# Scoring two head pairs at a time over four banks, projecting four pairs at a time, and a new order for the row

## Chip, cores and metric

The kernel runs on one core of one Trainium2 chip. The metric is the device time of one execution in microseconds (us). Engines are named as the profile names them: PE is TensorE, DVE VectorE, ACT ScalarE, POOL GpSimd, SP SyncE.

## The reference, cut to what matters

```python
x = L0_attn_x                                     # 16 rows (batches) of 256 tokens x 128
xn = _layernorm(x, axis=-1)
x = x + attention(xn) + experts(xn)
# attention: 16 heads of 8 channels
qkv = x @ Wqkv + bqkv
qf, kf = features(q), features(k)                 # normalised, times omega, clipped, exp: 64 features a head
ctx = einsum('bhtf,bhtfd->bhtd', q, cumsum(k v))  # causal linear attention
den = maximum(einsum(q, cumsum(k)), 1e-6)
out = (ctx / den) @ Wout + bout
# experts: 512 slots
logits = einsum('bsd,etd->bset', xn, se)
slots = softmax over tokens of logits, transposed, @ xn
processed = gelu(slots @ w1) @ w2
out = softmax over slots of logits @ processed
```

## The kernel before

One batch of 256 tokens is a *row* of the program; 16 rows are worked through, two of them before a hardware loop (`Fori`), twelve in it and two behind it (`run_rows`). Every engine has its instructions written out by hand in a function `row(b, first, nxt, nxt2)`; semaphores join them. `b` is the row, `bp` the one before, `b1` and `b2` the next two. Nothing reorders them: the order in which `row` is written is the order of each engine.

The causal attention is computed as scores: keys' features times queries' features, for eight *pairs* of heads a row (`scores(b, p)`, p from 0 to 7). One pair takes eight matmuls on a quarter of the array each (64 rows by 64 columns); head 0 of the pair goes to bank 0 of `p_s`, head 1 to bank 1. DVE takes bank 0 out with the causal mask (`evac_a`), ACT takes bank 1 out (`evac_b`), and POOL masks that one (`mask_b`). Then `context(b, a)` multiplies the scores with the values, on 128 by 32 tiles, into the last 128 columns of `p_s`; `ctx_copy`, `ctx_transposed`, `ctx_norm`, `attn_back`, `attn_copy`, `attention_out` and `add_attention` finish the attention.

`project(b, g)` makes the arguments of the features for two pairs, with fp16 operands on 64 by 128 tiles, into banks `p_f` and `p_g`; DVE clips them into `arg` (`clip`), ACT takes their exponential into `feat` (`feature_exp`), which has four places.

The expert part runs through four banks `x01` and `x23`: `logits_tokens`, `token_maxima`, `logits_turned`, `slot_maxima`, `shift`, `dispatch_exp`, `slot_sums`, `slots_norm`, `slots_transposed`, `slots_high` and `slots_low`, `hidden`, `gelu`, `processed`, `proc_copy`, `combine`, `add_experts`. They are full 128 by 128 matmuls, all but the bf16 ones of `shift` in fp32 or in an fp32 split in two. The layer norm and the qkv product of the next row use `x01` too.

In the row before the change one pair is scored at each of eight steps `s`, and a piece of the other work stands between one pair and the next:

```python
for s in range(8):
    ...
    scores(b, s)
    if s == 0:
        ... ctx_transposed(bp); qkv_product(b1)
    if s == 1:
        combine(bp); attn_back(bp)
```

Of the kernel before, what the change touches and what calls it, by code (L numbers as in the profile page):

```python
# [68 lines left out]
def step(b, k):  # L69

    i, u = b
    u += k
    return (i + u // 2, u % 2)

# [12 lines left out]
def build(nc, x, Wqkv, bqkv, Wout, bout, omega, nodes, weights, gamma_x, gamma_slot, slot_embeds,  # L87
          w1, w2, out):
    with ExitStack() as ctx:
# [81 lines left out]
        ffn_res = sb("ffn_res", [128, TILES, C])  # L171
# [112 lines left out]

        def load_omega(eng, a):
# [30 lines left out]
        def _(sp):  # L316
# [41 lines left out]
            load_x((0, 1), T)  # L358
            sp.wait_ge(om_zero, 1)
            load_omega(sp, 0)  # L360
            load_omega(sp, 1)
            spread(gs_bc, gamma_slot, C).then_inc(d_se, 16)
            sp.dma_start(se_rows[:, :, :], slot_embeds.rearrange("(c p) d -> p c d", p=128)).then_inc(d_se, 16)
# [9 lines left out]
            def row(b, first, nxt, nxt2):  # L373
                if nxt2:
                    load_x(step(b, 2), place(b, 2))
                if not first:
                    store(step(b, -1), place(b, -1))
                if nxt:
                    turn_stack(step(b, 1))

            run_rows(sp, row)
            store((B // 2 - 1, 1), (B - 1) * T)
# [7 lines left out]
        def _(pool):  # L390
# [63 lines left out]
            def row(b, first, nxt, nxt2):  # L454
                b1 = step(b, 1)
                for s in range(8):
                    if s == 2 and nxt:
                        squares(pool, b1)
                    if s == 4 and nxt:
                        qk_apply(pool, b1)  # L460
                    if s == 5 and nxt:
                        stack_low(pool, b1)
                    mask_b(b, s)
                    if s == 2 and nxt:
                        residual(b1)
                        place_v(b1)

            run_rows(pool, row)


        @block.scalar
        def _(act):
# [10 lines left out]
            def xt_high(b):  # L483
                after(act, tr_ok, count(b, 1, 1))
                nc.scalar.activation(xt_hi[:, b[1], :], x01[:, 0, 0:T], ACT.Copy).then_inc(xth_ok, 1)
# [17 lines left out]
            def evac_b(b, p):  # L503
                after(act, sb_ok, count(b, 8, p + 1))
                after(act, cx_ok, count(b, 4, p // 2 - 3))
                nc.scalar.activation(s_sb[:, p, 1, :], p_s[:, 1, 0:384], ACT.Copy).then_inc(eb_ok, 1)  # L506

            def ctx_copy(b, g):
                after(act, cx_ok, count(b, 4, 2 * g + 2))
                after(act, ct_ok, count(b, 1, 0))  # L510
                nc.scalar.activation(ctx_sb[:, g, :].rearrange("p (j t) -> p j t", j=TILES), p_s[:, :, 384:512],
# [24 lines left out]
            def proc_copy(b):  # L536
                after(act, pr_ok, count(b, 1, 1))
                nc.scalar.activation(proc[:, :, 0:C], x01[:, 1, :], ACT.Copy).then_inc(prs_ok, 1)  # L538
# [21 lines left out]
            qk_root(b0)  # L560

            stack_high(b0)
            nc.scalar.activation(stacked(2), parted(), ACT.Copy).then_inc(stcp_ok, 1)
# [5 lines left out]
            ln_root(b1)  # L569
# [3 lines left out]
            nc.scalar.activation(small[:, CT_, 8:12], small[:, CT_, 4:8], ACT.Exp, scale=-0.5).then_inc(se_a, 1)  # L573
            act.wait_ge(f_ok, 1)

            def row(b, first, nxt, nxt2):

                b1, b2, bp = step(b, 1), step(b, 2), step(b, -1)
                for s in range(8):
                    if s == 0:  # L580
                        if first:
                            feature_exp(b, 0)
                            act.wait_ge(se_t, 1)
                            nc.scalar.activation(se_hi[:, :], x23[:, 0, :], ACT.Copy).then_inc(se_h, 1)
                            feature_exp(b, 1)
                            xt_high(b1)
# [610 lines left out]
```

## Time and profile before

| | |
|---|---|
| median of 3 runs | 502.74 us (502.51 to 503.14) |
| time of the profiled execution | 502.99 us |
| span in its profile, first to last instruction | 501.0 us |
| PE busy | 466.5 us (93%) |
| DVE busy | 373.2 us (74%) |
| ACT busy | 312.8 us (62%) |
| POOL busy | 173.8 us (35%) |

The span is shorter than the time, since what lies around the first and the last instruction isn't in it. A PE busy time is modelled at its ends, so the start of a block of matmuls against the start of the next tells more than the sum.

### The profile page before, as it was taken

Reading aid. Unit: us, or ns where it says so; the run is one execution under the profiler, and the core shown is the slowest. Engines: PE = TensorE matmul, PEld = TensorE weight load, DVE = VectorE, ACT = ScalarE, POOL = GpSimd, SP = SyncE. Lnnn points to the kernel's source line nnn. Section 1 sums busy time; section 2 is a strip of 40 time slices with the busy share of each in tenths; the row PEclk is TensorE's granted clock in tenths of the full one; section 3 lists DMA queues with packets and bytes.
Section 4 is the critical chain, followed back from the end, with each engine's and each line's share of the span. In section 5 each row is a group of like instructions: output and inputs, shape, how many; then the busy total and the mean of one; then the engine's idle time right before and its main releaser. Section 6 shows DMA issues by size and latency. Waiting matters only on the chain.

```text
span 501.0 us, 15989 instructions
## 1 busy us (share of the span) xinstructions
PE 466.5 (93%) x5716; PEld 368.2 (73%) x5716; DVE 373.2 (74%) x985; ACT 312.8 (62%) x545; POOL 173.8 (35%) x277
## 2 busy tenths in 40 slices
PE   4559999999999999999999999999999999999996
PEld 2236777878777787877778787777778787777775
DVE  3887777787868778786877878787777878785651
ACT  3343848576574847667484766758485675758561
POOL 4324143341615334251523425161442426143210
PEclk9977999999999999999999999999999999999999
DMA  2500303040020202011020202002020200202000
GB/s 61 134 0 4 53 12 54 1 56 13 16 50 10 52 6 57 0 32 31 10 52 10 52 0 52 11 10 52 10 52 0 58 5 10 44 12 43 12 3 10
DMA packets 45779, 14.46 MB, mean 29 GB/s; under 512 B 35640, under 2 KB 45624, under 8 KB 45752
## 3 DMA queue, kind: packets, MB, share of 16 engines
q1 hardware_dynamic: 45176, 13.77, 13.9%
q8 instruction: 17, 0.28, 0.2%
q10 hardware_dynamic: 576, 0.33, 0.2%
q14 instruction: 10, 0.08, 0.1%
HBM read 3.61 MB, written 2.10 MB: 11 GB/s over the span
## 4 chain that ended last, share of the span: by engine, by line
PE 80%; DVE 9%; issue 5%; ACT 4%; DMA 1%; ACTq 0%; DVEq 0%
PE x L920 17%; PE p_s L958 14%; PE x L1074 13%; PE x L1085 6%; PE x L1047 6%; PE p_s L976 6%; PE p_f L945 4%; PE x L1019 4%; DVE log_sb L738 3%; ACT disp L521 3%; PE x L1030 3%; DVE arg L704 2%; PE x L999 2%; PE x L1055 2%; PE x L987 2%
## 5 line engine op out<-in xcount | busy, mean ns | idle before, releaser
L442 POOL TENSOR_TENSOR s_sb<-s_sb,causal 128x256 f32<-128x256 f32 x128 | 94.2, 736 | 281.9 <-ACT s_sb L506 281.9
L710 DVE TENSOR_TENSOR s_sb<-p_s,causal 128x384 f32<-128x384 f32 x128 | 71.2, 556 | 63.2 <-PE p_s L958 60.7
L958 PEld LDWEIGHTS p_s<-feat 64*64 64x64 f32 x2048 | 78.6, 134 | 35.9 <-issue 29.1
L958 PE MATMUL p_s<-feat 64*64 64x256 f32 (+3 forms) x2048 | 100.8, 313 | 1.1 <-DVE s_sb L710 1.1
L506 ACT ACTIVATE s_sb<-p_s 128x384 f32<-128x384 f32 x128 | 62.5, 488 | 50.8 <-PE p_s L958 50.2
L501 ACT ACTIVATE feat<-arg,f_bias 128x512 f32<-128x512 f32 x128 | 88.2, 713 | 4.3 <-DVE arg L704 4.3
L1074 PE MATMUL x<-w_sb,hid_t 128*128 128x128 f32 x512 | 65.7, 281 | 0.0
L704 DVE TENSOR_SCALAR arg<-p_f,f_low,f_high 128x512 f32<-128x512 f32 x64 | 51.6, 806 | 18.1 <-PE p_f L945 18.0
L1074 PEld LDWEIGHTS x<-w_sb,hid_t 128*128 128x128 f32 x512 | 59.6, 191 | 7.1 <-issue 7.0
L704 DVE TENSOR_SCALAR arg<-p_g,f_low,f_high 128x512 f32<-128x512 f32 x64 | 51.4, 803 | 0.0
L976 PE MATMUL p_s<-s_sb,vw 128*32 128x128 f32 x1536 | 48.6, 274 | 0.2
L976 PEld LDWEIGHTS p_s<-s_sb,vw 128*32 128x32 f32 x1536 | 40.3, 110 | 7.1 <-DVE s_sb L710 3.6
L475 ACT ACTIVATE small<-small 128x4 f32<-128x4 f32 (+1 forms) x32 | 7.4, 231 | 46.2 <-DVE small L691 39.8
L1047 PE MATMUL x<-xg,disp 128*128 128x129 f32 x256 | 32.8, 281 | 3.0 <-ACT disp L521 3.0
L1047 PEld LDWEIGHTS x<-xg,disp 128*128 128x128 f32 x256 | 29.8, 191 | 5.4 <-ACT disp L521 5.4
L1085 PE MATMUL x<-proc,comb_t 128*128 128x129 f32 x256 | 32.9, 281 | 0.2 <-ACT proc L538 0.2
L533 ACT ACTIVATE hid_t<-x 128x1024 f32<-128x1024 f32 x32 | 32.6, 1020 | 0.0
L1085 PEld LDWEIGHTS x<-proc,comb_t 128*128 128x128 f32 x256 | 29.8, 191 | 1.7 <-ACT proc L538 0.5
L945 PE MATMUL p_f<-stack_t,omega_st 64*128 64x512 f16 x64 | 24.5, 383 | 6.9 <-DVE arg L704 3.8
L920 PE MATMUL x<-slot_hi,w_hi 128*128 128x512 f32 x64 | 28.6, 447 | 0.0
L738 DVE TENSOR_SCALAR_CACHE_REDUCE log_sb<-x 128x512 f32<-128x512 f32 x32 | 21.4, 690 | 5.4 <-PE x L920 5.4
L920 PE MATMUL x<-slot_hi,w_lo 128*128 128x512 f32 x64 | 25.4, 397 | 0.0
(135 smaller groups left out, 798.4 us busy)
## 6 DMA issues: line engine op xcount, KB each, us to landing
out_dram<-out_sb SPq DMA_DIRECT2D x32, 64.0 KB, 2.1
xin<-in_L_attn_x_dram SPq DMA_DIRECT2D x31, 64.0 KB, 2.4
omega_f<-in_L_attn_omega_dram SPq DMA_DIRECT2D x16, 4.0 KB
se_rows<-n_L_ffn_slot_embeds_dram SPq DMA_DIRECT2D x1, 256.0 KB, 4.1
w_f<-in_L_ffn_w_dram SPq DMA_DIRECT2D x1, 256.0 KB, 4.3
w_sb<-in_L_ffn_w_dram SPq DMA_DIRECT2D x1, 256.0 KB, 4.7
stack_t<-stack SPq DMA_TRANSPOSE x16, 4.4
wqkv_f<-in_L_attn_Wqkv_dram SPq DMA_DIRECT2D x1, 192.0 KB, 3.9
```

Source lines behind the costliest of these rows:

```text
L442: pool.tensor_tensor(v, v, m, ALU.mult).then_inc(mb_ok, 1)
L501: nc.scalar.activation(feat[:, p % 4, :], arg[:, p % 4, :], ACT.Exp, bias=f_bias[:, 0:1]).then_inc(fe_ok, 1)
L506: nc.scalar.activation(s_sb[:, p, 1, :], p_s[:, 1, 0:384], ACT.Copy).then_inc(eb_ok, 1)
L704: nc.vector.tensor_scalar(arg[:, p % 4, :], bank[:, :], f_low[:, 0:1], f_high[:, 0:1], ALU.max, ALU.min).then_inc(cl_ok, 1)
L710: nc.vector.tensor_tensor(s_sb[:, p, 0, :], p_s[:, 0, 0:384], causal[:, :], ALU.mult).then_inc(ea_ok, 1)
L920: mm = nc.tensor.matmul(dst, a, w, start=start and i == 0, stop=stop and i == 2, skip_group_check=True)
L945: nc.tensor.matmul(bank[:, :], omega_st[rows, g, :], stack_t[rows, b[1], :, :, g, :].rearrange("p j k t -> p k j t"), start=True, stop=Tru ...
L958: mm = nc.tensor.matmul(p_s[rows:rows + 64, u, o:o + hi - lo], f[:, T + keys:T + keys + 64], f[:, lo:hi], start=True, stop=True, skip_grou ...
L976: mm = nc.tensor.matmul(p_s[32 * q:32 * q + 32, j, 384:512], vw[:, b[1], kt, QUADS * a + q, :], s_sb[:, p, q % 2, o:o + 128], start=(kt == ...
L1047: mm = nc.tensor.matmul(x01[:, half, 129 * (c % 2):129 * (c % 2) + 129], disp[:, j, 128 * c:128 * c + 128], xg[:, b[1], j, :], start=(j == ...
L1074: mm = nc.tensor.matmul(x01[:, 1, 128 * c:128 * c + 128], hid_t[:, m, 128 * c:128 * c + 128], w2_sb[:, m, :], start=(m == 0 and c == 0), s ...
L1085: mm = nc.tensor.matmul(x23[:, 0, 129 * j:129 * j + 129], comb_t[:, c, 128 * j:128 * j + 128], proc[:, c, :], start=(c == 0), stop=(c == N ...
```

## The change

Banks `p_f` and `p_g` go; in their place stands a second pair of score banks, `p_t`. Even pairs are scored into `p_s`, odd ones into `p_t`, two pairs one behind the other. Two projections also stand one behind the other, into the same four banks. Contexts go to `p_s`, `x23` or `x01` (`home`). The row now begins with the logits, the last two pairs of a row are scored in the next row, its contexts also; the experts of a row are finished in the row itself. `dispatch_exp` and `proc_copy` are cut in two halves, the qkv product goes to `x23`, results wait in a doubled `ffn_res`, and stores go out a row later. The start has its loads and steps in another order, and the layer norm of row 0 no longer stands behind the wait for the bias rows (`d_rows`).

```diff
-        p_f = pb("p_f", [128, 512])
-        p_g = pb("p_g", [128, 512])
         p_s = pb("p_s", [128, 2, 512])
+        p_t = pb("p_t", [128, 2, 512])
...
+        def home(b, g):
+
+            if g == 1:
+                return x23
+            return x01 if is_row(b, B - 1) else p_s
...
             def dispatch_exp(b):
-                after(act, shd_ok, count(b, 1, 1))
-                nc.scalar.activation(disp[:, :, :], x01[:, :, :], ACT.Exp).then_inc(ed_ok, 1)
+                for j in range(TILES):
+                    after(act, shd_ok, count(b, 2, j + 1))
+                    nc.scalar.activation(disp[:, j, :], x01[:, j, :], ACT.Exp).then_inc(ed_ok, 1)
...
             ln_stats(b0)
-            dve.wait_ge(d_rows, 32)
             ln_apply(b0)
...
             def project(b, g):
                 after(pe, d_st, count(b, 16, 16))
-                hold(pe, cl_ok, count(b, 8, 2 * g))
-                for u, (bank, done) in enumerate(((p_f, ft_ok), (p_g, fg_ok))):
+                if g == 0:
+                    hold(pe, ea_ok, count(b, 8, -1))
+                    hold(pe, eb_ok, count(b, 8, -1))
+                    hold(pe, cs_ok, count(b, 2, -1))
...
+                else:
+                    hold(pe, ea_ok, count(b, 8, g + 1))
+                    hold(pe, eb_ok, count(b, 8, g + 1))
...
             def scores(b, p):
                 after(pe, fe_ok, count(b, 8, p + 1))
-                after(pe, ea_ok, count(b, 8, p))
-                hold(pe, eb_ok, count(b, 8, p))
-                if p in (0, 6):
-                    hold(pe, cs_ok, count(b, 2, p // 6))
+                if p in (0, 1, 4, 5):
+                    hold(pe, cl_ok, count(b, 8, (2, 4, 0, 0, 6, 8)[p]))
+                else:
+                    hold(pe, ea_ok, count(b, 8, p - 1))
+                    hold(pe, eb_ok, count(b, 8, p - 1))
+                dst = (p_s, p_t)[p % 2]
...
-                for s in range(8):
...
+                logits_tokens(b, nxt)
+                if first:
+                    transposes(b1)
+                else:
+                    scores(bp, 6)
+                    scores(bp, 7)
+                logits_turned(b)
+                if not first:
+                    lump_low(bp, False)
+                shift(b)
+                if first:
+                    pe.wait_ge(om_s, 3)
+                project(b, 0)
+                project(b, 1)
+                slot_sums(b, 0)
+                slot_sums(b, 1)
+                if nxt:
+                    qkv_product(b1)
+                slots_transposed(b)
+                scores(b, 0)
+                scores(b, 1)
+                if not first:
+                    lump_high(bp, nxt, False)
+                if first:
+                    pe.wait_ge(w1_split, 2)
+                    pe.wait_ge(d_late, 16 * LATE)
+                hidden(b, first, 0)
+                hidden(b, first, 1)
+                scores(b, 2)
+                scores(b, 3)
+                processed_low(b)
+                if not first:
+                    ctx_transposed(bp)
+                project(b, 2)
+                project(b, 3)
+                processed_high(b)
+                if not first:
+                    attn_back(bp)
+                combine(b)
+                if not first:
+                    attention_out(bp)
+                if nxt2:
+                    transposes(b2)
+                scores(b, 4)
+                scores(b, 5)
```

`lump_low` is `context(b, 0)` and `context(b, 1)` with their waits, `lump_high` is `context(b, 2)` and `context(b, 3)`. `processed_low` and `processed_high` are the two halves of `processed`.

Two places show what moves. On PE before, inside a row of the loop, the second half of `processed` (L1074) stands ahead of pair 0 (the four rows of L958), and behind it the context transposes of the previous row (L987).

```order
L1074 MATMUL x01<-w2_sb,hid_t 128x128 x8
L53 REGISTER_ALU
L958 MATMUL p_s<-feat 64x256 x2
L958 MATMUL p_s<-feat 64x192 x2
L958 MATMUL p_s<-feat 64x64 x2
L958 MATMUL p_s<-feat 64x128 x2
L987 MATMUL x23<-ident,ctx_sb 128x128 x4
```

On PE of the change, from the end of pair 2 on: L989 are the matmuls of a pair (pair 3 goes to `p_t`), L1136 the first half of `processed`, L1043 the context transposes, L974 the projections.

```order
L989 MATMUL p_s<-feat 64x128 x2
L989 MATMUL p_t<-feat 64x256 x2
L989 MATMUL p_t<-feat 64x192 x2
L989 MATMUL p_t<-feat 64x64 x2
L989 MATMUL p_t<-feat 64x128 x2
L53 REGISTER_ALU
L1136 MATMUL x01<-w2_sb,hid_t 128x128 x8
L53 ISA
L53 REGISTER_ALU
L1043 MATMUL x23<-ident,ctx_sb 128x128 x4
L974 MATMUL p_s<-stack_t,omega_st 128x512 x2
L974 MATMUL p_t<-stack_t,omega_st 128x512 x2
```

Two pairs of heads now have nothing between them, and the projections stand two and two.

On DVE before, in the loop, the context normalisation of the previous row (L717 to L729) stands between two evacuations (L710), and the clips (L704) are spread over the row.

```order
L710 TENSOR_TENSOR s_sb<-p_s,causal 128x384
L53 ISA
L717 TENSOR_SCALAR den<-x 128x2x4x2 x2
L722 RECIPROCAL rden<-den 128x32
L53 REGISTER_ALU
L729 TENSOR_TENSOR attn<-x,rden 128x2x32 x4
L710 TENSOR_TENSOR s_sb<-p_s,causal 128x384
```

On DVE of the change the same normalisation (L744 to L756) stands ahead of four clips in a row (L730), the experts' sum (L796, L800), the low half of the transposed tokens (L698), the final addition (L808) and the evacuations of pairs 4 and 5 (L736).

```order
L756 TENSOR_TENSOR attn<-x,rden 128x2x32 x4
L53 REGISTER_ALU
L730 TENSOR_SCALAR arg<-p_s,f_low,f_high 128x512 x2
L53 REGISTER_ALU
L730 TENSOR_SCALAR arg<-p_t,f_low,f_high 128x512 x2
L796 RECIPROCAL comb_rs<-x 128x2
L800 SCALAR_TENSOR_TENSOR ffn_res<-x,comb_rs,xres 128x128 x2
L53 ISA
L698 TENSOR_TENSOR xt_lo<-x,xt_hi 128x256
L53 REGISTER_ALU
L808 TENSOR_TENSOR out_sb<-x,ffn_res 128x256
```

What was spread over the eight steps of a row now stands in one run of DVE, behind the normalisation.

## Rows read from the trace of the kernel before

**Rows 1.** The page, busy times by engine, and the chain by engine.

```profile
PE 466.5 (93%) x5716; PEld 368.2 (73%) x5716; DVE 373.2 (74%) x985; ACT 312.8 (62%) x545; POOL 173.8 (35%) x277
...
PE 80%; DVE 9%; issue 5%; ACT 4%; DMA 1%; ACTq 0%; DVEq 0%
```

**Rows 2.** Windows: length; PE, PEld, DVE, ACT, POOL busy; granted clock; DMA.

```profile
32.50:42.80 10.30, 8.05 (x61) 6.22 (x61) 6.55 (x14) 2.98 (x7) 4.41 (x8) 0.50 0.01 2
...
231.55:260.36 28.81, 28.21 (x357) 22.49 (x358) 22.66 (x60) 19.21 (x34) 10.51 (x16) 1.00 0.13 27
```

**Rows 3.** Timeline of PE, in one row of the loop: start, length, instructions.

```profile
241.20 0.77 PE L958 MATMUL p_s<-feat 64*64 64x256 f32 x16
241.90 0.71 PE L999 MATMUL x<-wout_sb,attn_t 128*128 128x128 f32 x4
...
243.60 0.40 PE L920 MATMUL x<-se_hi,xt_lo 128*128 128x512 f32 x1
243.93 0.77 PE L958 MATMUL p_s<-feat 64*64 64x256 f32 x16
244.80 1.09 PE L1019 MATMUL x<-ident,log_sb 128*128 128x128 f32 x8
245.82 0.39 PE L945 MATMUL p_f<-stack_t,omega_st 64*128 64x512 f16 x1
...
246.24 0.40 PE L1030 MATMUL x<-neg_ident,maxima 128*128 128x128 bf16 x4
...
247.38 0.77 PE L958 MATMUL p_s<-feat 64*64 64x256 f32 x16
...
251.79 1.52 PE L976 MATMUL p_s<-s_sb,vw 128*32 128x128 f32 x48
253.24 0.50 PE L920 MATMUL x<-slot_hi,w_hi 128*128 128x512 f32 x1
253.57 0.39 PE L920 MATMUL x<-slot_lo,w_hi 128*128 128x512 f32 x1
253.80 0.40 PE L920 MATMUL x<-slot_hi,w_lo 128*128 128x512 f32 x1
...
258.16 2.05 PE L1074 MATMUL x<-w_sb,hid_t 128*128 128x128 f32 x16
260.05 0.38 PE L928 MATMUL x<-ident,xg 128*128 128x128 f32 x2
260.36 0.39 PE L945 MATMUL p_f<-stack_t,omega_st 64*128 64x512 f16 x1
...
260.68 1.52 PE L976 MATMUL p_s<-s_sb,vw 128*32 128x128 f32 x48
```

**Rows 4.** Timeline of DVE, in the same row of the loop.

```profile
257.96 0.56 DVE L710 TENSOR_TENSOR s_sb<-p_s,causal 128x384 f32<-128x384 f32 x1
258.43 0.80 DVE L704 TENSOR_SCALAR arg<-p_f,f_low,f_high 128x512 f32<-128x512 f32 x1
259.15 0.80 DVE L704 TENSOR_SCALAR arg<-p_g,f_low,f_high 128x512 f32<-128x512 f32 x1
```

**Rows 5.** Timeline of ACT: the load of the other activation table.

```profile
259.43 1.28 ACT L622 ACT_TABLE_LOAD   x1
```

**Rows 6.** Waits of PE from 60 to 460 us: total, times, longest.

```profile
PE p_f L945 <- DVE arg L704: 3.8, 12, 0.4
```

**Rows 7.** Timeline of DVE at the start.

```profile
8.18 0.16 DVE L636 SCALAR_TENSOR_TENSOR small<-small 128x4 f32<-128x4 f32 x1 [3.50 <-DMA bqkv_bc<-in_L_attn_bqkv_dram]
```

**Rows 8.** Timeline of SP at the start: the omega loads.

```profile
8.59 5.64 SPq L292 DMA_DIRECT2D omega_f<-in_L_attn_omega_dram  x16
```

**Rows 9.** The line of the slot transposes: durations, first and last start.

```profile
L1055 PE MATMUL x<-ident,slot_v x64: 272/273/330, 49.2 to 481.3; 128*128 128x128 f32 x64
```

**Rows 10.** Timeline of PE in the last row: slot transposes and context transposes.

```profile
480.90 0.66 PE L1055 MATMUL x<-ident,slot_v 128*128 128x128 f32 x4
...
492.94 0.60 PE L987 MATMUL x<-ident,ctx_sb 128*128 128x128 f32 x4
```

More of the change, by code:

```diff
@@ L376, in row @@
                 if not first:
-                    store(step(b, -1), place(b, -1))
-                if nxt:
-                    turn_stack(step(b, 1))
+                    turn_stack(b)
+                if not first and not is_row(b, 1):
+                    store(step(b, -2), place(b, -2))
             run_rows(sp, row)
-            store((B // 2 - 1, 1), (B - 1) * T)
+            for u in range(2):
+                store((B // 2 - 1, u), (B - 2 + u) * T)
             for u in range(2):
@@ L681, in qkv_bias @@
                     after(dve, qkv_ok, count(b, 2, j + 1))
-                    last = nc.vector.scalar_tensor_tensor(qkv[:, j, :], x01[:, j, 0:384], small[:, SG, j:j + 1],
+                    last = nc.vector.scalar_tensor_tensor(qkv[:, j, :], x23[:, j, 0:384], small[:, SG, j:j + 1],
                                                           bqkv_bc[:, :], ALU.mult, ALU.add)
@@ L840, in _ @@
             last.then_inc(se_ok, 1)
-            clip(b0, 0)
-            clip(b0, 1)
+            ln_stats(b1)
+            dve.wait_ge(om_s, 2)
+            for u in range(2):
+                o = 64 * u
+                last = nc.vector.tensor_tensor(omega_st[o + 32:o + 48, :, :], omega_f[o:o + 16, :, :],
+                                               omega_st[o:o + 16, :, :], ALU.subtract)
+            last.then_inc(om_s, 1)
+            dve.wait_ge(f_ln, 1)
+            nc.vector.tensor_tensor(f_bias[:, :], coef_ln[:, :], node_c[:, :], ALU.subtract).then_inc(f_ok, 1)
@@ new lines, in row @@
+                evac_a(b, 1)
+                if nxt:
+                    qk_norms(b1)
+                    qk_newton(b1)
+                if nxt2:
+                    ln_apply(b2)
+                if nxt:
+                    stack_again(b1)
+                evac_a(b, 2)
+                evac_a(b, 3)
+                if not first:
+                    ctx_norm(bp)
+                clip(b, 4)
+                clip(b, 5)
+                clip(b, 6)
+                clip(b, 7)
+                add_experts(b)
@@ L1023, in logits_turned, with shift @@
                         mm.then_inc(lt_ok, 1)
-            def shift(b, h):
-                after(pe, mx_ok, count(b, 2, h + 1))
-                for c in (2 * h, 2 * h + 1):
-                    for j in range(TILES):
+            def shift(b):
+                after(pe, mx_ok, count(b, 2, 2))
+                for j in range(TILES):
+                    for c in range(NCH):
                         mm = nc.tensor.matmul(x01[:, j, 128 * c:128 * c + 128],
@@ L1056, in slots_transposed, with hidden @@
                 mm.then_inc(slt_ok, 1)
-            def hidden(b, nxt, half):
+            def hidden(b, first, half):
                 if half == 0:
@@ L1061, in hidden @@
                     after(pe, slh_ok, count(b, 1, 1))
+                elif not first:
+                    after(pe, cs_ok, count(b, 2, 0))
                 else:
-                    after(pe, ec_ok, count(b, 1, 1))
+                    pe.wait_ge(qkvs_ok, 2)
                 for m in (2 * half, 2 * half + 1):
@@ L1097, in _ @@
             qkv_product(b0)
-            pe.wait_ge(sthi_ok, 1)
-            for u in (0, 1, 0, 1, 0, 1):
-                nc.tensor.matmul(p_s[:, u, 0:384], ident[:, :], s_sb[:, 0, 0, :], start=True, stop=True)
-            pe.wait_ge(om_s, 3)
-            project(b0, 0)
             pe.wait_ge(se_ok, 1)
             for c in range(NCH):
-                mm = nc.tensor.transpose(x23[:, 0, 128 * c:128 * c + 128], se_n[:, c, :], ident[:, :])
+                mm = nc.tensor.transpose(x01[:, 1, 128 * c:128 * c + 128], se_n[:, c, :], ident[:, :])
```

477 lines of the change are left out of this document (230 added, 247 removed).

## The prediction

> **What bounds the kernel now.** I read the page first: PE is busy for 93% of the span and is 80% of the chain that ended last [rows 1]. The windows show one row of the loop, 28.81 us long: PE is busy 28.21 us of it at the full clock, DVE 22.66, ACT 19.21, POOL 10.51 [rows 2]. PE's waits are small: for the clips 3.8 us in all between 60 and 460 us [rows 6]. So the kernel is PE's list of blocks, 16 times over, and only what shortens that list or empties it can move the time. From the slot transposes of the first row (49.2, [rows 9]) to those of the last (480.9, [rows 10]) are 15 periods of 28.78 us.
>
> The timeline of PE tells what a block costs beside its columns [rows 3]. A run of 128 by 128 matmuls goes at a steady step: 16 instructions from 258.16 to 260.05, 1.89 us for 8 matmuls of 128 columns, 1.84 ns a column with the start. But each time the kind of tile changes there is a loss. The first split matmul behind a context takes 0.33 us (253.24 to 253.57), the next 0.23: entering costs 0.10. The last one ahead of a pair takes 0.33 too (243.60 to 243.93): leaving costs 0.10 (rounded down to 0.09 in the sums). A row of before has 25 such changes of kind, since eight pairs, four projections and two contexts all stand apart in the full-width work; a row of the change has 15.
>
> **The sum for a row.** The same matmuls run, so I lay their measured pieces end to end in the new order. Pieces that have a row [rows 3]: turned logits 1.02 (244.80 to 245.82), shift 1.14 (246.24 to 247.38), a context of two groups 1.45 (251.79 to 253.24), a lone pair of heads 0.70 (241.20 to 241.90), a lone projection 0.32 (260.36 to 260.68). The others follow from 0.235 for a 512-column split instruction, three quarters of it for a 384-column one, 0.11 for half a fp32 matmul of 128 columns, and 0.10 each for entering and leaving.
> - logits 1.60; turned 1.02; context 1.45; shift 1.14
> - slot sums, qkv product, slot transposes in one run: 1.78 + 1.04 + 0.44 + 0.19 = 3.45
> - context 1.45; both hidden halves in one run, 12 x 0.235 + 0.19 = 3.02
> - first half of processed with context transposes, 1.78 + 0.44 + 0.19 = 2.42 (rounded up)
> - second half, attention back, combine, attention out, transposes: 1.78 + 0.22 + 1.78 + 0.45 + 0.22 + 0.19 = 4.64
>
> Together 20.19 us. To it come four double pairs and two double projections. The trace never shows two blocks of one kind with a wait between them, so the second block's price is bounded. For a pair: below, the lone block without its two ends, 0.70 - 0.19 = 0.51; above, everything paid again, 0.70 + 0.19 = 0.89. Each quarter of the array streams 320 columns in a pair (256 + 64, 192 + 128), at 1.84 ns 0.59 us; I take 0.60. For a projection: below 0.13, above 0.51; 512 columns in one pass are the 0.23 of a split instruction, which I take. So 4 x (0.70 + 0.60) + 2 x (0.32 + 0.23) = 6.30, and the row is 26.5 us.
>
> The Trainium skill (TensorEngine Tiling (Array Packing), Key Properties) says that a change of tiling mode drains TensorE and that going to another tile of one mode does not. The 0.10 on either side agree with it; by it the second block of a pair pays nothing, which is the 0.60, while with both switches paid again the sum would be 502 (worked out below).
>
> **Who is late next.** I walked the other engines through this row from its logits (0), with DVE steps of 0.47 for an evacuation and 0.72 for a clip [rows 4], 1.28 for each of the two table loads [rows 5], and what the same line took before for the rest. One place makes PE wait. The slot sums need both halves of the dispatch exponential, done at 7.0, and run to 8.95; DVE, with three clips ahead (to 9.1) and then both normalisations (to 10.3), frees the slot transposes only at 10.4, when the qkv product, which covers 1.0 of it, has ended at 10.0. That is 0.4 us a row. Elsewhere the cover holds, thinly: fourth clip 11.0 for pair 1 at 11.6; qkv bias 12.1 for the context at 12.25, where the array goes into `x23`; evacuation of pair 3 at 19.7 for the projection at 20.5, behind a table load and both GELUs on ACT; proc halves 22.5 and 23.7 for the combine at 23.2 and 24.0; all four later clips 24.8 for pair 5 at 26.3; pair 5 out of its bank 1.2 us into the next row, for pair 7 at 2.2. POOL and SP are not near: the stack of a row goes out at 19.2 of the row before and has some 14 us until its projections. Splitting the dispatch exponential and the proc copy costs ACT one more small start each, within its idle time of 9.6 us (28.81 - 19.21, [rows 2]). So the row is 26.93 us, and 15 periods are 404.0 against 431.7. Three joints with 0.1 to 0.3 us in hand will slip at times; for these I add 0.2 a row, 3 us in all.
>
> **The two ends.** Start: the norm of row 0 no longer waits for the bias rows, 3.5 us of DVE idle [rows 7]. The logits no longer stand behind the first projections and their transposing DMA, but behind the normalised slots. The sixteen omega loads took 5.64 us to issue [rows 8]; they now start some 3.5 us earlier, ahead of the load of the second row, so the slot rows are asked for at about 11 and land at about 15. Behind that stand on ACT their squares and both roots, on DVE the query and key norms, the stack and the normalised slots, at 21.7 by their lengths; then the transposes and the warm-up matmuls, so the logits start at about 26 and the slot transposes at 35.4, one row's chain later, with waits; I say 37, since part of it may run at half clock, as 32.5 to 42.8 us does now [rows 2]. Before it was 49.2 [rows 9]. Tail: before, 20.1 us from the last slot transposes to 501.0 [rows 10]. Now almost all of the attention lies behind them: 1.30 + 1.45 + 3.02 + 1.30 + 2.42 + 0.55 + 4.4 + 1.30 for the rest of the row, 1.45 and 1.30 for the first contexts and pairs 6 and 7, 0.55 for the slot transposes, 1.5 for the last evacuation and mask, 1.45 for the last context, 0.6 for its copy, and 7.4 from the context transposes on (8.06 from 492.94 to 501.0, less 0.7 since the combine isn't between): 30.1.
>
> **Sum:** 37.0 + 404.0 + 3.0 + 30.1 = 474.1 us of span. The profiled execution lasted 502.99 us with a span of 501.0, so 2.0 us lie around it: 476 us. Its time is 0.25 above the median of 502.74, which I leave out.
>
> **Rivals.**
> - *The evacuations bind* (0.20). DVE must put 22.66 us into 26.9, and what was spread over eight steps stands in one run: context normalisation, four clips, experts' sum, low half, addition, evacuations. If DVE keeps the scattered idle of before, 28.81 - 22.66 = 6.15, nothing is won; if half of what should go (1.9 us) stays, the row is 27.9 and the time 491. For it: 0.1 to 0.5 us in hand at several joints. Against: each wait here is for work that is one block old. The Trainium skill (TensorEngine Tiling (Array Packing), PSUM Bottleneck) warns that with a tiled array the copies out of PSUM may become the limit, and asks for both engines on it, as both kernels have; it would give this case.
> - *The change doesn't save its switches* (0.07). If the wait ahead of the second block lets the array run empty, each second pair costs 0.89 and each projection 0.51: 15 x (4 x 0.29 + 2 x 0.28) = 26 us, time 502, no change; half of it gives 489. Against: the conditions are usually met before the wait is reached.
> - *The clock falls* (0.06), the slower side. In 32.5 to 42.8 us PE was busy 8.05 of 10.3 us and granted 0.50 of its clock [rows 2]. If the wait ahead of the slot transposes brought that on, a microsecond there would do half the work. The 27 us forecast are eaten by about 54 us at half clock, 3.6 a row; one stretch of 5 us a row would give 476 + 15 x 2.5 = 514. Against: in the loop the full clock is granted [rows 2], and the new wait is 0.4 us.
>
> **How the numbers follow.** The forecast case has 0.67 and spans 468 (second pair at 0.51, no slips: 4 x 0.09 x 15 + 3 = 8 less) to 484 (second pair 0.7 and another slip of 0.1 a row). The range takes in most of the evacuation case: 468 to 492. About 0.2% tells from no change. Faster is the forecast case, the evacuation case and most of the second rival: 0.91; same 0.03; slower 0.06.
>
> **What would show it.** In the profile after: slot transposes 26.9 to 27.2 apart; the second pair starts 0.70 behind the first and the next kind 0.60 behind that; PE's waits led by the slot transposes for `slot_v`, some 6 us; first slot transposes near 37. Wrong, if PE's waits for `s_sb`, `arg` or `feat` exceed 10 us, if the clock shows 0.5 inside the loop, or if the second pair takes 0.8 or more.

## The result

| | before | the change |
|---|---|---|
| median | 502.84 us (502.51 to 503.14, 4 runs) | 474.38 us (474.12 to 476.84, 4 runs) |
| profiled execution: time, span | 502.99, 501.0 us | 476.84, 475.1 us |

The ratio is 0.9445 [0.9418, 0.9472]: 28.5 us less. The forecast was 476 us, in a range of 468 to 492. The profiled execution of the change is the slowest of its four, 2.5 us above their median, and everything read from the profile below is from that one.

### The profile page after: what moved, and what is told of

Read it like the earlier page. It is cut to its first block, busy times and chain, and to the rows that moved or that the text cites. A ratio compares the mean times of both kernels' runs of the same rounds, so it can differ in the third digit from the quotient of the medians.

```text
span 475.1 us, 16056 instructions
## 1 busy us (share of the span) xinstructions
PE 438.9 (92%) x5712; PEld 361.6 (76%) x5712; DVE 388.5 (82%) x985; ACT 307.0 (65%) x578; POOL 171.1 (36%) x277
## 4 chain that ended last, share of the span: by engine, by line
PE 80%; DVE 12%; issue 4%; SPq 2%; DMA 1%; ACT 1%; DVEq 0%
PE x L936 16%; PE p_s L989 9%; PE p_t L989 7%; PE x L1136 7%; PE x L1145 7%; PE x L1157 6%; DVE arg L730 6%; PE x L1001 5%; PE p_s L1001 5%; PE x L1079 3%; DVE slot_v L785 3%; PE p_s L974 2%; PE x L1114 2%; PE x L1090 2%; PE x L1055 2%
## 5 line engine op out<-in xcount | busy, mean ns | idle before, releaser
L730 DVE TENSOR_SCALAR arg<-p_s,f_low,f_high 128x512 f32<-128x512 f32 x64 | 48.8, 803 | 18.0 <-PE p_s L974 18.0
L989 PEld LDWEIGHTS p_s<-feat 64*64 64x64 f32 x1024 | 38.6, 132 | 18.2 <-issue 16.6
L730 DVE TENSOR_SCALAR arg<-p_t,f_low,f_high 128x512 f32<-128x512 f32 x64 | 50.0, 801 | 0.0
L989 PE MATMUL p_s<-feat 64*64 64x256 f32 (+3 forms) x1024 | 49.5, 309 | 0.0
L989 PE MATMUL p_t<-feat 64*64 64x256 f32 (+3 forms) x1024 | 46.1, 296 | 0.0
L527 ACT ACTIVATE s_sb<-p_s 128x384 f32<-128x384 f32 x64 | 31.0, 484 | 21.2 <-PE p_s L989 21.2
L989 PEld LDWEIGHTS p_t<-feat 64*64 64x64 f32 x1024 | 41.5, 133 | 1.5
L736 DVE TENSOR_TENSOR s_sb<-p_s,causal 128x384 f32<-128x384 f32 x64 | 35.2, 550 | 6.6 <-PE p_s L989 5.8
L736 DVE TENSOR_TENSOR s_sb<-p_t,causal 128x384 f32<-128x384 f32 x64 | 35.1, 548 | 0.0
L1136 PE MATMUL x<-w_sb,hid_t 128*128 128x128 f32 x256 | 32.8, 281 | 0.0
L527 ACT ACTIVATE s_sb<-p_t 128x384 f32<-128x384 f32 x64 | 31.5, 493 | 0.7
L1136 PEld LDWEIGHTS x<-w_sb,hid_t 128*128 128x128 f32 x256 | 29.8, 191 | 1.2
```

Of the source, the lines that this page charges most:

```text
L527: nc.scalar.activation(s_sb[:, p, 1, :], (p_s, p_t)[p % 2][:, 1, 0:384], ACT.Copy).then_inc(eb_ok, 1)
L730: nc.vector.tensor_scalar(arg[:, p % 4, :], bank, f_low[:, 0:1], f_high[:, 0:1], ALU.max, ALU.min).then_inc(cl_ok, 1)
L736: nc.vector.tensor_tensor(s_sb[:, p, 0, :], (p_s, p_t)[p % 2][:, 0, 0:384], causal[:, :], ALU.mult).then_inc(ea_ok, 1)
L989: mm = nc.tensor.matmul(dst[rows:rows + 64, u, o:o + hi - lo], f[:, T + keys:T + keys + 64], f[:, lo:hi], start=True, stop=True, skip_grou ...
L1136: nc.tensor.matmul(x01[:, c // 2, o:o + 128], hid_t[:, m, 128 * c:128 * c + 128], w2_sb[:, m, :], start=(m == 0 and c % 2 == 0), stop=Fals ...
```

## The profile after

The page: busy times by engine, to be held against [rows 1].

```profile
PE 438.9 (92%) x5712; PEld 361.6 (76%) x5712; DVE 388.5 (82%) x985; ACT 307.0 (65%) x578; POOL 171.1 (36%) x277
```

PE has the same matmuls, less four instructions of warm-up at the start (which write nothing that is read), and is busy 27.6 us less. Nearly all of that is in the loop: 28.21 us busy in a row of before [rows 2], 26.39 in the row below. The columns are the same, so what went lies between the blocks of matmuls, where the profile counts it as busy. DVE has the same 985 instructions and is busy 15.3 us more. That is the line of this page to stop at: equal work that takes longer calls for a reason.

The line of the slot transposes (against [rows 9]; its last start is that of the row's last matmul), and then windows: most of one loop row, the stretch at half clock in the first row, and everything from the last row's slot transposes on.

```profile
L1114 PE MATMUL x<-ident,slot_v x64: 272/273/331, 39.0 to 444.9; 128*128 128x128 f32 x64
```

```profile
43.50:46.90 3.40, 3.40 (x9) 2.62 (x10) 2.62 (x9) 1.79 (x3) 0.73 (x2) 0.50 0.00 0
231.04:257.84 26.80, 26.39 (x356) 21.92 (x348) 23.52 (x61) 18.44 (x36) 10.14 (x16) 1.00 0.14 29
444.56:475.10 30.54, 22.76 (x360) 19.11 (x360) 12.49 (x33) 14.95 (x26) 5.66 (x8) 0.92 0.04 10
```

The first transposes start at 38.98 and the last row's at 444.56: 15 periods of 27.04 us, where before had 28.78. So the span is 38.98 + 405.58 + 30.54 = 475.1, and 1.7 us lie around it. The start is 10.2 us shorter than before and the tail 10.4 us longer, so by the profiles the whole gain of the span, 26 us, is in the rows.

PE's timeline in one row of the loop (start, length, instruction, in brackets the idle time before it), to be held against [rows 3].

```profile
235.24 0.77 PE L989 MATMUL p_s<-feat 64*64 64x256 f32 x16
235.84 0.72 PE L989 MATMUL p_t<-feat 64*64 64x256 f32 x16
236.49 2.05 PE L1136 MATMUL x<-w_sb,hid_t 128*128 128x128 f32 x16
238.38 0.60 PE L1043 MATMUL x<-ident,ctx_sb 128*128 128x128 f32 x4
239.13 0.39 PE L974 MATMUL p_s<-stack_t,omega_st 64*128 64x512 f16 x2 [0.16 <-issue]
239.59 0.39 PE L974 MATMUL p_t<-stack_t,omega_st 64*128 64x512 f16 x2
239.92 2.05 PE L1145 MATMUL x<-w_sb,hid_t 128*128 128x128 f32 x16
...
252.11 0.39 PE L974 MATMUL p_s<-stack_t,omega_st 64*128 64x512 f16 x2
252.33 0.38 PE L974 MATMUL p_t<-stack_t,omega_st 64*128 64x512 f16 x2
...
255.52 0.34 PE L936 MATMUL x<-wqkv_hi,xt_lo 128*128 128x384 f32 x1
256.01 0.66 PE L1114 MATMUL x<-ident,slot_v 128*128 128x128 f32 x4
256.59 0.77 PE L989 MATMUL p_s<-feat 64*64 64x256 f32 x16
```

Read the starts. Two pairs take 0.60 (235.24 to 235.84) + 0.65 (to 236.49) = 1.25 us. The slot transposes start 0.49 behind the last matmul of the qkv product, which steps at 0.18: a wait of 0.31. And projection 3 starts 0.46 behind projection 2 (239.13 to 239.59), where projection 1 starts 0.22 behind projection 0 (252.11 to 252.33). Projection 2 is late too. From the context transposes to the second half of `processed` it is 1.54 us here (238.38 to 239.92), and 1.07 in the kernel with the copy moved, below (260.42 to 261.49). That is a loss of 0.47 us in this row and 0.54 in the next, which the prediction does not have. The idle time in the brackets, 0.16, is less than the wait of projection 2, since PE's ends are modelled.

What makes these projections late? Projection 2 goes into `p_s` and waits for the evacuation of pair 2, projection 3 into `p_t` and waits for that of pair 3. Here is DVE at the same place of the next row, then ACT's evacuation of pair 3, and the two projections.

```profile
262.09 1.02 DVE L660 SCALAR_TENSOR_TENSOR small<-small 128x4 f32<-128x4 f32 x1 [0.22 <-DVE small L664]
...
264.51 1.06 DVE L777 COPY stack<-stack 128x512 f16<-128x512 f16 x1
265.50 0.55 DVE L736 TENSOR_TENSOR s_sb<-p_s,causal 128x384 f32<-128x384 f32 x1
265.97 0.54 DVE L736 TENSOR_TENSOR s_sb<-p_t,causal 128x384 f32<-128x384 f32 x1
...
265.12 0.51 ACT L527 ACTIVATE s_sb<-p_t 128x384 f32<-128x384 f32 x1
...
266.25 0.39 PE L974 MATMUL p_s<-stack_t,omega_st 64*128 64x512 f16 x2 [0.23 <-issue]
266.71 0.39 PE L974 MATMUL p_t<-stack_t,omega_st 64*128 64x512 f16 x2
```

Each projection starts 0.20 us behind the end of its evacuation on DVE (266.05 and 266.51). ACT's of pair 3 has ended at 265.63, 0.88 us earlier than DVE's. So it is DVE that holds them, and on DVE the copy of the stack (L777) stands right ahead.

POOL in that row:

```profile
262.01 1.08 POOL L313 TENSOR_TENSOR qk_n<-qkv,small 128x512 f32<-128x512 f32 x1 [1.55 <-DVE small L664]
264.27 1.16 POOL L321 TENSOR_TENSOR stack<-qk_n,stack 128x512 f16<-128x512 f32 x1 [1.18 <-ACT stack L516]
```

An operation on four elements a partition takes 1.02 us and ends when POOL's does (263.11 and 263.09). The fp16 copy takes 1.06 us, and ends 0.14 behind POOL's `stack_low`, which is running when it starts. It is so in 12 of the 15 copies (1.06 to 1.10 us; the first two and the last take 0.28 to 0.30) and in 12 of the 16 small operations. The twelve rows with a long copy have projections 2 and 3 at 0.46 to 0.49 us apart. The three with a short copy, and the last row, which has none, have them 0.22 to 0.23 apart. The groups by line, after:

```profile
L777 DVE COPY stack<-stack 128x512 f16<-128x512 f16 x15 | 13.9, 924 | 2.2 <-ACT stack L516 2.2
L660 DVE SCALAR_TENSOR_TENSOR small<-small 128x4 f32<-128x4 f32 x16 | 12.9, 809 | 3.2 <-DVE small L664 2.6 <-ACT small L497 0.5
```

And before, the same two operations:

```profile
L750 DVE COPY stack<-stack 128x512 f16<-128x512 f16 x15 | 5.2, 348 | 0.0
L636 DVE SCALAR_TENSOR_TENSOR small<-small 128x4 f32<-128x4 f32 x16 | 2.5, 154 | 3.7 <-DMA bqkv_bc<-in_L_attn_bqkv_dram 3.5 <-ACT small L477 0.2
```

8.7 and 10.4 us more: together more than all of DVE's growth, 15.3. The Trainium skill ("SBUF — State Buffer", Who interferes with whom) says that GpSimd and some operations of VectorE share an access to SBUF that one of them holds for its whole instruction. The trace agrees, with 1.02 us for an operation of 0.15 to 0.16, which starts 0.08 behind POOL's and ends with it.

The two operations also overlapped before, without a price for DVE. Here are the copy and POOL's `stack_low` in the row of [rows 3]:

```profile
250.09 0.28 DVE L750 COPY stack<-stack 128x512 f16<-128x512 f16 x1
...
250.23 1.16 POOL L310 TENSOR_TENSOR stack<-qk_n,stack 128x512 f16<-128x512 f32 x1 [0.32 <-ACT stack L495]
```

In 14 of 15 rows of before the copy starts 0.05 to 0.20 us ahead of POOL's and takes 0.28; in the one where POOL is ahead, by 0.05, it takes 1.25. In the twelve long rows of the change POOL is ahead by 0.21 to 0.25. So it is not the overlap that counts but which of the two starts first: against POOL's start the copy comes 0.3 to 0.45 us later in the change than before. (In two rows of the change POOL's start is recorded 0.02 ahead and the copy is still short.)

## The experiments

Each time is a median with its range; the ratio is to the kernel before, run beside it. "Row" is the period of the slot transposes.

### The pairs apart again

The change, with three of the four pairings undone; pairs 0 and 1 stay together.

```diff
                     scores(bp, 6)
-                    scores(bp, 7)
                 logits_turned(b)
                 if not first:
+                    scores(bp, 7)
                     lump_low(bp, False)
...
                 hidden(b, first, 0)
-                hidden(b, first, 1)
                 scores(b, 2)
+                hidden(b, first, 1)
                 scores(b, 3)
...
                 combine(b)
+                scores(b, 4)
                 if not first:
                     attention_out(bp)
...
-                scores(b, 4)
                 scores(b, 5)
```

> The change with three of the four double pairs taken apart: turned logits between pairs 6 and 7, the first hidden half... the second hidden half between pairs 2 and 3 (pair 2 stands between the two hidden halves), attention out and transposes between pairs 4 and 5. Banks, waits and matmuls are the same. Theory (the gain is the changes of tile kind saved): each adds one lone block, 0.19 us of entering and leaving and 0.65 to 0.70 in place of 0.60 behind the first, so 0.24 to 0.29 us each, three a row, 16 rows: 11.5 to 14 us slower than the change, 486 to 488 us. Rival (the gain came from waits that the new order hides, not from the tile kinds): within 2 us of the change.

Measured: 499.99 us (498.43 to 501.46), ratio 0.9945 [0.9922, 0.9968], row 28.53. That is 25.6 us against the change, twice what the theory had, and the rival doesn't have it either. PE's waits of this kernel between 60 and 440 us (total, times, longest) show why.

```profile
PE x L1090 <- DVE maxima L772: 5.8, 14, 0.4
PE x L936 <- DVE xt_lo L698: 2.5, 6, 0.4
PE x L936 <- issue: 1.9, 7, 0.3
```

The edit opened two waits: the shift for the maxima, 0.4 us a row, and the logits for `xt_lo`, 0.3 to 0.4 a row, since less PE work now stands ahead of both. So this run can't price a pairing. It was split in two further down.

### The copy behind the evacuations; the normalisations ahead of the clip; both

Three kernels, each the change with one or both of two moves on DVE. The copy of the stack is let past the two evacuations that projections 2 and 3 wait for:

```diff
-                if nxt:
-                    stack_again(b1)
                 evac_a(b, 2)
                 evac_a(b, 3)
+                if nxt:
+                    stack_again(b1)
```

> The change with the second copy of the stack on DVE (1.06 us here, 0.28 before) moved behind the evacuations of pairs 2 and 3. Theory: projections 2 and 3 wait about 0.4 us a row for DVE's evacuations of pairs 2 and 3, which stand behind that copy while POOL works; moving it frees them: 15 x 0.4 = 6 us faster than the change, about 468.5. Rival: ACT's evacuations of the same pairs, behind both GELUs, come as late, so at most 1.5 us faster. Second rival: what starts earlier stalls at the next joint, no change.

Measured: 468.90 us (468.75 to 470.28), ratio 0.9349 [0.9319, 0.9379], row 26.56, 5.5 us less than the change, as the theory had it (its row is 0.48 shorter, of which 0.07 is the half clock in the first row of the change, which this kernel did not have). PE's timeline at the projections:

```profile
260.95 0.39 PE L974 MATMUL p_s<-stack_t,omega_st 64*128 64x512 f16 x2
261.18 0.38 PE L974 MATMUL p_t<-stack_t,omega_st 64*128 64x512 f16 x2
261.49 2.05 PE L1145 MATMUL x<-w_sb,hid_t 128*128 128x128 f32 x16
```

They are 0.23 apart, and the next kind starts 0.31 behind: 0.54 for both. The copy itself fell too, since in most rows POOL's `stack_low` has ended when it comes, or ends within 0.03 us.

```profile
L777 DVE COPY stack<-stack 128x512 f16<-128x512 f16 x15 | 4.6, 307 | 0.0
```

The second move goes for the wait that the prediction did have:

```diff
                 clip(b, 1)
-                clip(b, 2)
                 slots_norm(b, 0)
                 slots_norm(b, 1)
+                clip(b, 2)
                 clip(b, 3)
```

> The change with both slot normalisations on DVE ahead of the third clip. Theory: the slot transposes no longer wait (0.32 us a row in the loop), the fourth clip comes 0.1 us later and pair 1 waits at most 0.15: 0.2 to 0.3 a row, 3 to 4.5 us faster, 470 to 471.5. Rival: pair 1 or the context behind it takes the whole wait over, since the fourth clip and the qkv bias are late next: no change within 1 us.

Measured: 476.76 us (475.78 to 478.58), ratio 0.9508 [0.9471, 0.9545], row 27.08: nothing won. The row is 0.04 longer, and the 2.4 us that the median is above the change's are no clear loss, since the ranges and the intervals of the two overlap. PE's timeline:

```profile
254.35 0.34 PE L936 MATMUL x<-wqkv_hi,xt_lo 128*128 128x384 f32 x1
254.53 0.60 PE L1114 MATMUL x<-ident,slot_v 128*128 128x128 f32 x4
255.05 0.78 PE L989 MATMUL p_s<-feat 64*64 64x256 f32 x16
255.88 0.78 PE L989 MATMUL p_t<-feat 64*64 64x256 f32 x16
256.84 1.52 PE L1001 MATMUL x<-s_sb,vw 128*32 128x128 f32 x48 [0.18 <-DVE qkv L707]
```

The transposes start at once (0.18), but pair 1 starts 0.83 behind pair 0 instead of 0.60, behind the clips, and the context waits for the qkv bias. DVE's work between the slot sums and that context is one sum; its order only chooses who stands at the end of it.

> Both of the DVE moves in one kernel. Theory: they stand at different joints and add up: 9 to 10.5 us faster than the change, 464 to 465.5. Rival: PE's list is at its floor of 26.5 us a row, so the sum of both can be no more than 15 x 0.55 = 8 us, 466.

Measured: 473.24 us (472.06 to 474.14), ratio 0.9418 [0.9387, 0.9449]. The steady row is 26.77, against 26.56 with the copy's move alone, so the second move costs 0.2 a row once the first is made; its first row also lasted 29.36 us, with 42.2 to 49.1 us at half clock, against 26.97. The gains don't add.

### The start, on the kernel with the copy moved

The warm-up matmuls left out (they write nothing that is read):

```diff
-            for u in (0, 1, 0, 1):
-                nc.tensor.matmul(p_s[:, u, 0:384], ident[:, :], s_sb[:, 0, 0, :], start=True, stop=True)
```

> The kernel with the stack copy moved (468.9 us), without the four warm-up matmuls ahead of row 0's logits. Theory (they only keep the array busy and are in the way): the low halves of the slots are done at 26.8 us and the logits start at 28.7 to 29.2, so 1.9 to 2.4 us faster, 466.7. Rival: the array is then granted half its clock in the first row, where a 512-column instruction steps 0.43 in place of 0.23 us, and the first row is longer by more than that: same or up to 5 us slower.

Measured: 469.73 us (467.76 to 470.09), ratio 0.932 [0.9279, 0.9362]. No difference from the kernel with them that these ranges can tell. PE's timeline without:

```profile
27.57 0.77 PE L936 MATMUL x<-se_hi,xt_hi 128*128 128x512 f32 x1 [2.29 <-issue]
28.14 0.63 PE L936 MATMUL x<-se_lo,xt_hi 128*128 128x512 f32 x1
28.56 0.63 PE L936 MATMUL x<-se_hi,xt_lo 128*128 128x512 f32 x1
```

And with them:

```profile
28.67 0.69 PE L936 MATMUL x<-se_hi,xt_hi 128*128 128x512 f32 x1
29.20 0.40 PE L936 MATMUL x<-se_lo,xt_hi 128*128 128x512 f32 x1
29.43 0.40 PE L936 MATMUL x<-se_hi,xt_lo 128*128 128x512 f32 x1
```

Without them the logits start 1.1 us earlier and step at 0.43, with them later and at 0.23. Either way the slot transposes come at about 38: at 38.6 without, at 38.1 with, and at 37.4 to 39.0 over all the kernels here that have the warm-ups. In this profile the first row without them also lasted 27.83 us, with half clock from 42.5 to 46.0, against 26.97; the change itself, with the warm-ups, had such a stretch too, so it can't be put down to them.

The wait for the bias rows put back where it was before the change:

```diff
             ln_stats(b0)
+            dve.wait_ge(d_rows, 32)
             ln_apply(b0)
```

> The kernel with the stack copy moved, with the wait for the bias rows put back ahead of the layer norm of row 0. Theory: the start now hangs on the slot rows, for which ACT waits until 16.7 us, and what is moved by 1.2 to 2.9 us at the start ends well before: no change, within 1 us of 468.9. Rival (the removed wait is part of the gain): 1.2 to 2.9 us slower.

Measured: 469.91 us (467.62 to 470.74), ratio 0.9339 [0.9303, 0.9376]. No difference, although the same wait was DVE's longest at the start before [rows 7].

### More work on DVE

One more clip a row (0.72 us, to a place that nobody reads) ahead of the eighth clip, on the kernel with the copy moved. It tests whether DVE's sum of work is near to binding.

```diff
+                if p == 7:
+                    nc.vector.tensor_scalar(junk[:, :, :].rearrange("p a c -> p (a c)"), bank, f_low[:, 0:1],
+                                            f_high[:, 0:1], ALU.max, ALU.min)
```

> The kernel with the stack copy moved, with one clip more a row on DVE (0.72 us, its result goes nowhere), ahead of the eighth. Theory (DVE has 1.0 to 1.4 us in hand at the end of a row): 0 to 0.2 a row, at most 3 us slower, 472. Rival (the evacuations bind): 16 x 0.72 = 11.5 us slower, 480.

Measured: 468.57 us (467.79 to 470.73), ratio 0.9321 [0.928, 0.9362], row 26.56. It costs nothing at that place. The stretch ahead of the slot transposes, where DVE is what PE waits for, isn't tested by it.

### Prices of single pairings, on the kernel with the copy moved

Half of `processed_high` (`processed_high(b, h)` does chunks 2h and 2h + 1) between the second two projections:

```diff
                 project(b, 2)
+                processed_high(b, 0)
                 project(b, 3)
-                processed_high(b)
+                processed_high(b, 1)
```

> The kernel with the stack copy moved, with the first half of the second half of processed between projections 2 and 3. Theory (a change of tile kind costs what it did for the pairs): a lone projection costs 0.32 in place of 0.22 and 0.19 for entering and leaving, 0.29 a row, 4.6 us slower, 473.5. Rival (the later projection makes clips, features and pair 5 late): 10 us or more slower, with waits of PE at pair 5 or at the next row's logits.

Measured: 473.45 us (472.3 to 474.97), ratio 0.9413 [0.937, 0.9457], row 26.85: 0.29 a row.

The second half of `hidden` between pairs 2 and 3:

```diff
-                hidden(b, first, 1)
                 scores(b, 2)
+                hidden(b, first, 1)
                 scores(b, 3)
```

> The kernel with the stack copy moved (468.9 us, row 26.55), with only pairs 2 and 3 taken apart by the second hidden half. Theory (of the 1.5 us a row that taking three pairs apart cost, 0.35 each is tile kinds: two lone pairs 1.41 with 0.19 more of entering and leaving, against 1.25 for a double one; the rest is waits at other joints): row 26.9, 5 us slower, 474. Rival (each separation costs a third of the 1.5): row 27.05, 7.5 us slower, 476.5.

Measured: 474.44 us (473.24 to 476.06), ratio 0.9447 [0.9406, 0.9488], row 26.89: 0.33 a row, with no other wait of note.

Pair 4 ahead of `attention_out` and the transposes:

```diff
+                scores(b, 4)
                 if not first:
                     attention_out(bp)
                 if nxt2:
                     transposes(b2)
-                scores(b, 4)
                 scores(b, 5)
```

> The same with only pairs 4 and 5 taken apart, attention out and the transposes of row b+2 between them. Theory: 0.35 of tile kinds, and the transposes now stand 0.7 us later, so xt_high and xt_low are late for the next row's logits: 0.35 + 0.4 a row, row 27.3, 11 us slower, 480, with PE waiting for xt_low. Rival (no such wait when only this one is apart): 5 us slower, 474.

Measured: 480.35 us (479.11 to 480.71), ratio 0.9556 [0.9524, 0.9589], row 27.26: 0.70 a row. The logits now wait for `xt_lo`, by PE's timeline:

```profile
246.71 0.49 PE L936 MATMUL x<-se_hi,xt_hi 128*128 128x512 f32 x1 [0.42 <-DVE xt_lo L698]
```

So 0.70 is a pairing of 0.3 and a wait of 0.4. With this and the run before it the first experiment is explained: three pairings at 0.34, 0.4 for the maxima and 0.4 for `xt_lo` make 1.8; of the projections' wait, by starts 0.47 and 0.54 in turn, 0.10 and 0.18 to 0.19 are left, so about 0.3 a row goes off, which leaves 1.5 against the 1.49 measured.

### Where the copy's price comes from

Moving the copy on DVE changed two things, its place and its neighbour on POOL. Two kernels keep DVE's list of the change and reorder POOL's alone. In the first the copy of v goes ahead:

```diff
-                    stack_low(pool, b1)
                     place_v(b1)
+                    stack_low(pool, b1)
```

> The change itself, DVE as it was, with POOL's placing of the values ahead of its low half of the stack, so that a copy and no two-input operation runs on POOL when DVE comes to the second stack copy. Theory (DVE's copy takes 0.92 us on average since it has to let POOL's two-input operation end): the copy takes about 0.3 us again, projections 2 and 3 no longer wait, about 5 us faster than the change, 469 to 470. Rival (it is its place in DVE's order, or the wait for ACT's stack, that costs): the copy still ends after 0.9 us or the projections still wait, within 1 us of 474.4.

Measured: 475.74 us (474.76 to 476.85), ratio 0.9477 [0.9431, 0.9522], row 27.03. POOL in this kernel:

```profile
262.58 0.77 POOL L446 COPY vw<-qkv 128x64 f32<-128x64 f32 x4
263.83 1.16 POOL L321 TENSOR_TENSOR stack<-qk_n,stack 128x512 f16<-128x512 f32 x1 [0.47 <-ACT stack L516]
```

and DVE:

```profile
264.06 1.07 DVE L777 COPY stack<-stack 128x512 f16<-128x512 f16 x1
```

The copy of v fell into time in which POOL had idled for ACT, so `stack_low` still starts just ahead of DVE's copy. The collision was not removed, and the run decides nothing. In the second, `stack_low` goes behind two masks that can only run once ACT's evacuations are there:

```diff
-                    stack_low(pool, b1)
                     place_v(b1)
                 mask_b(b, 2)
                 mask_b(b, 3)
+                if nxt:
+                    stack_low(pool, b1)
```

> This is the change as made, with GpSimd's list alone in another order: the copy of v, then the masks of pairs 2 and 3, and only behind them the low half of the query and key stack. VectorE's list stays as in the change, with its repeat of the stack's first half ahead of the evacuations of pairs 2 and 3. Nothing is then left for GpSimd to run at the moment when that copy comes. Theory (the copy is slow because it shares an access to SBUF with an operation of GpSimd): the copy falls from 924 ns to about 0.3 us, projections 2 and 3 start 0.22 apart without a wait, the row is about 26.65 and the time about 469 to 470 us. Rival (the copy's place in VectorE's own list, or its wait for ScalarE's half of the stack, is what costs): copy and time stay, 0.92 us and 474.4 us.

Measured: 470.75 us (468.02 to 471.27), ratio 0.9383 [0.9333, 0.9433], row 26.56. DVE's group of the copy, at its old place in DVE's list (one line further down in this file):

```profile
L778 DVE COPY stack<-stack 128x512 f16<-128x512 f16 x15 | 4.2, 283 | 2.2 <-ACT stack L517 2.2
```

POOL's timeline around the copy, which ran at 259.26:

```profile
257.78 0.77 POOL L446 COPY vw<-qkv 128x64 f32<-128x64 f32 x4
260.13 1.41 POOL L454 TENSOR_TENSOR s_sb<-s_sb,causal 128x256 f32<-128x256 f32 x2 [1.58 <-ACT s_sb L528]
261.50 1.17 POOL L321 TENSOR_TENSOR stack<-qk_n,stack 128x512 f16<-128x512 f32 x1
```

The copy takes 283 ns at the same place and with the same wait for ACT, because POOL runs nothing then; the projections are 0.23 apart (260.68 and 260.91) and the row is that of the kernel with the copy moved. The theory is right: the price of the copy was POOL's operation, not its place on DVE.

## Why the prediction was right, and where it was off

**What bounds the kernel** was right: PE's list of blocks. The row's own terms add up to 26.89 where the prediction writes 26.93, and the tail's to 30.0 where it writes 30.1; neither matters to the time. With the copy moved, PE is busy for 26.42 of a 26.60 us stretch of the loop.

**The second pair** was given 0.60 and the next kind 0.10 less than a lone pair. The second starts 0.60 behind the first, so the first doesn't pay the 0.10 that a lone pair pays on leaving, and the next kind starts 0.65 behind the second: 1.25 instead of 1.30 for both, 0.2 us a row. "The second pair starts 0.70 behind the first" was thus wrong by 0.10. A pairing saves 0.33 a row by the one run that undid one without opening a wait, a pairing of projections 0.29.

**The stall at the slot transposes** was given as 0.4 a row and is 0.31, for the reason given. The sign that it was to be PE's first wait in the list, with some 6 us, did not come: the list has 0.3 us for it and 2.2 for the projections between 60 and 440 us, since the modelled ends of PE hide waits this short; by the starts it is 0.31 x 15 = 4.6. Undoing it moved it to pair 1 and the context.

**The step that failed** is the walk's "evacuation of pair 3 at 19.7 for the projection at 20.5, behind a table load and both GELUs on ACT". Its 0.8 us in hand were on ACT's side; DVE's side, with the copy of the stack right ahead of both evacuations, was not looked at, and the copy was taken at its length of before. ACT came as forecast: its evacuation of pair 3 ended at 265.63, 19.8 behind the logits (245.81), but DVE's ended at 20.7. It cost 0.47 or 0.54 in each of twelve rows, or 0.40 a period over the fifteen, about 6 us; with the copy moved the time was 5.5 us less. The allowance of 0.2 a row for slips, the pairs' 0.2 and the 0.1 less at the slot transposes made up for it, so the row came out as 27.04 against 26.93 + 0.2. The sum was right because two errors met, and the number of the row alone would not have told so.

**The account of a row.** Undone one at a time the pairings give 4 x 0.33 + 2 x 0.29 = 1.9 (if those not undone singly are like those that were); the new waits take 0.40 + 0.31; PE's listed waits of before, 6.7 us in 60 to 440, or 0.5 a row, are gone. 1.9 - 0.7 + 0.5 = 1.7, and 28.78 - 27.04 is 1.74. They agree better than the terms are worth: a listed wait falls short of the one by starts, as at the projections above.

**The start** was given as 37.0 and is 38.98 (37.5 to 38.7 in the other kernels with this start). The transposes of the normalised slots, forecast at 21.7, started at 23.73, and the logits, forecast at 26, at 29.19: 5.46 for transposes and warm-ups, where the forecast had 4.3. The omega loads took longer to issue than [rows 8], and the slot rows are asked for behind them. SP's timeline:

```profile
5.33 7.62 SPq L303 DMA_DIRECT2D omega_f<-in_L_attn_omega_dram  x16
12.98 0.41 SPq L372 DMA_DIRECT2D se_rows<-n_L_ffn_slot_embeds_dram  x1
```

The reason given first, the norm of row 0 freed from the bias rows, was not what shortened the start: with that wait put back nothing is lost. What is left as the cause, by the same argument the order of the logits against the projections, was not tried alone. The half clock that the start was given some room for came in the first row (43.5 to 46.9), behind 2.46 us in which PE waited for `w_lo`; that row lasted 28.00.

**The tail** was given as 30.1 and is 30.54. The last 5.1 us run at a clock of 0.52, where the last attention matmuls took 1.22 us; before they took 0.71.

**The rivals.** *The evacuations bind*: the one stall that the prediction lacks is at an evacuation, but not for the reason in that rival. DVE's scattered idle was given up (23.52 us busy in 26.80), and 0.72 us more a row ahead of the eighth clip cost nothing. *The switches are not saved*: fell, with 0.60 to the second pair, and 0.33 when one is undone. *The clock falls*: in the loop 1.00 was granted, over the wait ahead of the slot transposes too.

**A better version** is either of the two that take the copy away from POOL's operation: 468.90 and 470.75 us, whose intervals overlap, both below the change.

## What to carry to other kernels

- When work moves, compare the mean length of each DVE and POOL operation before and after. Here the two that grew had started behind an operation of the other engine and ended with it, or 0.15 us behind. Look at which of the two starts first, also where they overlapped before without harm. It matters where something waits behind it: here moving either of the two bought 5.5 and 3.6 us, while the second collision of this kernel, with nothing late behind it, was left alone.
- Where PE binds and its blocks are of several kinds of tile, put those of one kind side by side: here 0.3 us for each joint that goes, as long as what each block waits for keeps its cover. An edit that undoes a pairing also opens waits; price one at a time.
- In a walk of waits, do every engine that a wait names, not the one that looks latest.

## What the runs showed of the hardware

- DVE's fp16 copy of 512 columns took 283 ns with POOL idle, 283 to 285 ns in the rows of before where it started 0.05 to 0.20 us ahead of POOL's fp32 to fp16 subtraction, and 1059 to 1103 ns where it started 0.21 to 0.25 behind. A DVE operation on 4 elements a partition took 1.02 us when it started 0.08 behind POOL's product of 512, where it takes 0.16. In the second case the operation ahead and the one behind keep their length.
- Leaving out the four warm-up calls (eight matmul instructions) before the first row changed the step of the logits (0.43 instead of 0.23 us) and not the time by more than the ranges (469.73 and 468.90 us).
- A lone 64 by 64 pair of heads lasts 0.70 us; two in a row 1.25, over two pairs of banks.
